# Overlapping the end of an FFN with the next block: per-sequence sum and LayerNorm inside the last attention slots, front of a state-space block beside the last MLP

## The chip, the cores and the metric

The kernel runs on one core of one Trainium2 chip. Its engines are TensorE (PE), VectorE (DVE), ScalarE (ACT), GpSimd (POOL) and SyncE (SP), which only issues DMAs here. They run their own instruction queues and meet at semaphores. The metric is the device time of one execution in microseconds; less is better.

## What is computed

Input x is 4 sequences of 512 tokens with 128 channels, all in f32. Four blocks follow one another, each with its own LayerNorm (without weights) and residual sum:

```python
x = x + gla(layernorm(x))       # gated linear attention
x = x + ffn(layernorm(x))       # the first FFN: 6 layers
x = x + mamba(layernorm(x))     # the state-space block
x = x + ffn(layernorm(x))       # the second FFN, same weights
```

A layer of the FFN, on its own stream x, is

```python
x = local_attention(shift_tokens(x)) @ Wo + x
xn = layernorm(shift_tokens(x)) * g + b
a, gate = split(xn @ W1 + b1)
x = (a * gelu(gate)) @ W2 + b2 + x
```

The state-space block, on the normed x, is

```python
x, z = split(x @ in_proj); x = silu(causal_conv4(x) + conv_b)
dt, B, C = split(x @ x_proj); delta = softplus(dt @ dt_proj + 2 * dt_b)
for each of 16 states n:  h = h * exp(delta * A[n]) + delta * x * B[n];  y += h * C[n]
out = ((y + x * D) * silu(z)) @ out_proj
```

## The kernel before

All activations lie transposed, channels on partitions and the tokens of a sequence along the row: `xm` (x_main) is the residual stream, `xf` (x_ffn) the stream of the running block, `[128, 4, 512]` each. The order of each engine's queue is written by hand; nothing is reordered.

**PSUM** has 8 banks of 512 f32: `proj_ps` (0, 1), `tr_ps` (2, 3), `s_ps` (4, 5), `o_ps` (6, 7). In the state-space block banks 6 and 7 are `front`, 0 and 1 hold the spread b, 3 the spread c, 2 and 0 or 1 the inputs, 4 and 5 the sums y.

**An FFN** is 24 iterations `it = 4 * layer + j` of a body over sequence j, and a body is four slots u = 0 to 3 of 128 tokens. The work is staggered: in slot u the q, k, v projections are those of slot u + 2 or u + 3, transposes and scores of slot u + 1, probs times values of slot u (`pe_pv`, L328), and the output projection of slot u - 1 (`pe_wo`, L363; `dve_wo` adds it to the stream). The MLP of the sequence before rides along: centering, variance and `act_rstd` in slot 0, the up projections (`pe_up`, L385 and L386) with gelu and `dve_hidden` in slots 1 and 2, the down projection (`pe_down`, L394, and `dve_down`) in slot 3. All of these use banks 6 and 7. The last body has no next slots to project, and after it come, by themselves, the last output projection and the whole MLP of sequence 3.

**The hand-over.** Then `dve_add(1)` adds `xf` to `xm` for four sequences (L1049), and `pe_ln`, `act_ln`, `dve_ln` with stage 2 normalize all four: centering (L987), square, one-column matmuls with the mean (L991), a square root on ACT (L1015), a reciprocal and a diagonal matrix on DVE (L1033, L1037), a matmul that spreads it (L997), the scale on DVE (L1028). SP fetches the state-space weights when the sums are done (L1189, L1191; 8 DMAs, `mamba_in` waits for them). POOL multiplies taps and input weights (L1491) and makes the skip diagonals (L1495).

**The state-space block** has a front for each sequence b: 8 convolution matmuls (L1209), silu into `mb_u` (L1317), two gate matmuls (L1216) and their silu (L1321), x_proj (L1223), the split of its result in three bf16 parts (`first_part`, `rest_part`, `middle_part`, `last_part`), dt_proj (L1232), and softplus by four rounds of a square on ACT (L1346) and a product on DVE (L1422). Then 16 steps n: PE spreads b and c (L1241, L1244), ACT makes the decay (L1360) and copies c (L1364), DVE makes the inputs (L1440) and scans (L1447), POOL multiplies by c (L1512), and PE sums (L1255). Step s = 16 b + n. The front of sequence b + 1 is worked off inside the steps of b: convolutions at n = 0, 2, 3, 4, gates at 5, silu on ACT after the decay and c of step 6 (the "silu visit"), x_proj at 6, dt_proj at 7.

In SBUF the FFN's and the state-space block's buffers share one region, one after the other.

## Time and profile before

| | |
|---|---|
| three runs | 3748.36, 3751.72, 3775.46 us |
| median | 3751.72 us |
| profiled execution | 3771.7 us, its span 3769.9 us |
| mean granted clock of TensorE | 0.967 |
| PE, DVE, ACT, POOL busy in the span | 92%, 78%, 72%, 72% |
| the stretch 1740 to 1764 us | DVE 5.26, ACT 5.54, POOL 0.00 us busy |

All times on the profile's clock are microseconds from the span's start. Busy time of PE is modelled and includes waiting in its pipeline. In a timeline, a row is one or several equal instructions, and the brackets say how long the engine had been idle before it and what released it. On PE a f32 matmul leaves two records, so x16 are eight matmuls. PEclk is the share of full clock that TensorE was granted: 1.00 is 2.4 GHz, 0.50 is 1.2 GHz.

### The profile page before, as it was taken

How to read it: one execution, taken by the hardware profiler on the slowest of the kernel's cores; microseconds unless marked ns; L12 is line 12 of the kernel's file. 1: busy time of each engine (PE TensorE's matmuls, PEld its weight loads, DVE VectorE, ACT ScalarE, POOL GpSimd, SP SyncE). 2: the span in 40 equal slices, each digit the busy share in tenths (PEclk: the TensorE clock that was granted, in tenths of full speed). 3: DMA queues.
4: the chain of work that ended last, by engine and by line, in shares of the span. 5: the costliest groups of instructions: out<-in, count | busy, mean ns of one | idle time of the engine just before them, and what ended most of it. 6: DMA issues, size and time to landing. Idle time of an engine off the chain costs nothing. (4 is left out here: it accounts for less than half of the span.)

```text
span 3769.9 us, 152591 instructions
## 1 busy us (share of the span) xinstructions
PE 3478.4 (92%) x62652; PEld 2492.0 (66%) x62652; DVE 2942.3 (78%) x4681; ACT 2729.4 (72%) x7144; POOL 2732.0 (72%) x3102
## 2 busy tenths in 40 slices
PE   8799999999999999997787799999999999999997
PEld 3477777777777777774232477777777777777774
DVE  7678888878878788783799688878888887878783
ACT  2477878777887778773656477877777787877774
POOL 4588878777878778781466587878787787878772
PEclk9899999999999999997899899999999999999998
DMA  1222333332333323221000133323332332323321
GB/s 41 57 74 74 80 77 76 80 77 70 84 77 75 80 72 81 75 73 40 0 1 1 45 76 74 84 74 76 78 77 72 84 79 68 87 72 76 77 73 37
DMA packets 182983, 252.03 MB, mean 67 GB/s; under 512 B 53396, under 2 KB 74520, under 8 KB 182168
## 3 DMA queue, kind: packets, MB, share of 16 engines
q1 hardware_dynamic: 182296, 242.31, 25.4%
q8 instruction: 500, 8.19, 1.0%
q14 instruction: 187, 1.53, 0.1%
HBM read 39.73 MB, written 1.05 MB: 11 GB/s over the span
## 5 line engine op out<-in xcount | busy, mean ns | idle before, releaser
L860 POOL TENSOR_TENSOR qk_rows<-rot_products 128x512 f32<-128x512 f32 x768 | 982.7, 1281 | 237.1 <-DVE rot_products L659 233.9
L659 DVE TENSOR_TENSOR rot_products<-psum,rot_scaled 128x1024 f32<-128x1024 f32 x768 | 936.7, 1220 | 156.8 <-ACT squares L470 132.9
L870 POOL TENSOR_TENSOR qk_rows<-qk_rows,rnorm 128x512 f32<-128x512 f32 x768 | 802.6, 1076 | 15.0
L266 PE MATMUL psum<-wqkv_hi,xs_hi 128*128 128x512 f32 x1152 | 561.0, 487 | 89.3 <-DVE rot_products L659 37.9
L470 ACT ACTIVATE squares<-psum 128x512 f32<-128x512 f32 x768 | 488.7, 637 | 46.1 <-PE psum L268 40.2
L661 DVE TENSOR_REDUCE sumsq<-squares 128x8 f32<-128x512 f32 x768 | 518.7, 675 | 0.0
L478 ACT ACTIVATE v_rows<-psum 128x512 f32<-128x512 f32 x384 | 228.2, 596 | 377.5 <-DMA v_pairs<-v_rows 203.2
L835 POOL TENSOR_TENSOR probs<-probs,rden 128x512 f32<-128x512 f32 x384 | 392.5, 1043 | 111.1 <-DVE rden L709 109.9
L328 PEld LDWEIGHTS psum<-probs_t,v_pairs 64*64 64x64 f32 x24576 | 394.0, 137 | 106.0 <-issue 105.5
L514 ACT ACTIVATE probs<-psum,minus_row_max 128x64 f32<-128x64 f32 x1536 | 458.7, 337 | 5.7 <-DVE minus_row_max L693 5.5
L268 PE MATMUL psum<-wqkv_hi,xs_lo 128*128 128x512 f32 x1152 | 461.4, 401 | 0.3 <-issue 0.3
L267 PE MATMUL psum<-wqkv_lo,xs_hi 128*128 128x512 f32 x1152 | 460.5, 400 | 0.0
L328 PE MATMUL psum<-probs_t,v_pairs 64*64 64x32 f32 x24576 | 421.4, 222 | 30.9 <-issue 27.2
L363 PEld LDWEIGHTS psum<-o_t,wo 128*128 128x128 f32 x3072 | 366.5, 194 | 87.6 <-ACT o_t L486 67.2
L363 PE MATMUL psum<-o_t,wo 128*128 128x128 f32 x3072 | 391.4, 281 | 28.5 <-ACT o_t L486 20.6
L279 PE MATMUL psum<-ident,qk_rows 128*128 128x128 f32 x3072 | 407.1, 276 | 0.7 <-ACT q_t L497 0.7
L279 PEld LDWEIGHTS psum<-ident,qk_rows 128*128 128x128 f32 x3072 | 362.1, 143 | 29.3 <-issue 3.4
L313 PEld LDWEIGHTS psum<-k_t,q_t 64*32 64x32 f32 x24576 | 268.5, 105 | 152.8 <-issue 152.7
L514 ACT ACTIVATION_READ_ACCUMULATOR probs<-psum,minus_row_max 128x1 f32 x1536 | 355.6, 231 | 0.0
L266 PEld LDWEIGHTS psum<-wqkv_hi,xs_hi 128*128 128x128 f32 x1152 | 219.3, 190 | 191.8 <-issue 115.3
L313 PE MATMUL psum<-k_t,q_t 64*32 64x64 f32 x24576 | 330.9, 224 | 1.6 <-issue 1.6
L693 DVE TENSOR_REDUCE minus_row_max<-psum 128x16 f32<-128x1024 f32 x192 | 234.3, 1221 | 113.3 <-PE psum L313 113.1
(163 smaller groups left out, 6020.9 us busy)
## 6 DMA issues: line engine op xcount, KB each, us to landing
v_pairs<-v_rows SPq DMA_DIRECT2D x3072, 64.0 KB, 2.0
wqkv_staged<-in_Wqkv SPq DMA_DIRECT2D x52, 384.0 KB, 3.8
wo<-in_Wo SPq DMA_DIRECT2D x12, 512.0 KB, 4.5
w<-in_W SPq DMA_DIRECT2D x12, 341.0 KB, 3.7
qk_scale<-in_qk_scale SPq DMA_DIRECT2D x12, 128.0 KB, 3.6
w<-in_W SPq DMA_DIRECT2D x12, 128.0 KB
rot_base<-in_rot SPq DMA_DIRECT2D x2, 512.0 KB, 3.7
mb_bc_pick<-in_mb_bc_pick SPq DMA_DIRECT2D x1, 1024.0 KB
```

The source lines that it names most:

```text
L266: nc.tensor.matmul(proj_ps[c % 2], xh, wh, start=True, stop=False)
L268: nc.tensor.matmul(proj_ps[c % 2], xl, wh, start=False, stop=True).then_inc(S["qkv_mm"], 1)
L279: last = nc.tensor.transpose(tr_ps[g % 2][:, i * P:(i + 1) * P], m["qk"][:, u % 2, (4 * g + i) * P:(4 * g + i + 1) * P], ident[:, :])
L313: last = nc.tensor.matmul(s_ps[par][WIN * w:WIN * w + WIN, 64 * hp:64 * hp + 64], m["qt"][rows, hp, WIN * w:WIN * w + WIN], m["kt"][rows, ...
L328: last = nc.tensor.matmul(o_ps[par][64 * j:64 * j + 64, P * (hp // 2) + WIN * w:P * (hp // 2) + WIN * w + WIN], m["vp"][rows, u % TILES, w ...
L363: last = nc.tensor.matmul(o_ps[0][:, 0:P], m["wo"][:, hp, :], m["ot"][:, hp, :], start=(hp == 0), stop=(hp == HP - 1))
L470: nc.scalar.activation(m["sq"][:, c % 2, :], proj_ps[c % 2], ACT.Square).then_inc(S["sq_done"], 1)
L514: last = nc.scalar.activation(m["p"][:, hp, 1, :], s_ps[1][:, 2 * WIN * hp:2 * WIN * (hp + 1)], ACT.Exp, bias=m["mx"][:, 1, hp:hp + 1], ac ...
L659: V.tensor_tensor(m["mm"][:, c % 2, :, :].rearrange("p a (h e) -> p a h e", e=DH), ps, cos_sin, ALU.mult)\
L661: V.tensor_reduce(m["ss"][:, HC * c:HC * c + HC], m["sq"][:, c % 2, :].rearrange("p (h e) -> p h e", e=DH), AX.X, ALU.add)\
L860: G.tensor_tensor(qk[:, c * CH:(c + 1) * CH].rearrange(half, a=2, e=DH // 2), cos, sin[:, :, ::-1, :], ALU.add)\
L870: G.tensor_tensor(part, part, m["rn"][:, u % 2, HC * c:HC * c + HC].unsqueeze(2) .to_broadcast([P, HC, DH]), ALU.mult).then_inc(S["rot_don ...
```

## The change

Sum and LayerNorm between the first FFN and the state-space block are done sequence by sequence, with new functions (`pe_norm_center`, `pe_norm_var`, `pe_norm_spread`, `act_norm_square`, `act_norm_seed`, `pool_norm`, `dve_sum`, `dve_norm_scale`). Those of sequence 0 stand in slots 2 and 3 of the last body, those of 1 and 2 among the tail of the FFN and the front of the state-space block, that of 3 in the first steps. The inverse square root is an Ln and an Exp of the four columns on ACT, one Newton step and the diagonal on POOL, in place of a square root on ACT and a reciprocal and a diagonal on DVE.

The output projection and MLP of the last sequence are interleaved with the front of sequence 0 of the state-space block, on banks 2 to 5, and the down and output projections in the last slot go to banks 5 and 4 behind the exponentials. The weights of the state-space block are fetched after the last k is transposed. In the block, silu stands in the middle of step 7 on ACT (in the decay, ahead of the copy of c), the gates with x_proj at step 6 on PE, `rest_part` and `last_part` one step later on DVE; for b = 0 the convolutions stand at steps 2 to 5. The weights, vectors, rotary tables, `o_t` and `xn_mlp` of the FFN keep their place for the whole kernel, the rotary base is loaded once, and `mb_tap_w` and `mb_dt_low` lie in other tiles. The functions of the block are renamed with `mb_`.

```diff
+            mb["wt"] = mb["taps"]
...
+            mb["xdt"] = mb["rest"][0:RANK, :]
...
+        tail_ps = ((s_ps[0], s_ps[1]), (tr_ps[0], tr_ps[1]), (s_ps[0], s_ps[1]))
...
+        def pe_norm_center(b, out):
+            nc.tensor.wait_ge(x_ready, 2 * B + b + 1)
+            wait(nc.tensor, ln_done[2], b)
+            nc.tensor.matmul(out, center[:, :], xm[:, b, :], start=True, stop=True).then_inc(N["center_mm"], 1)
+
+        def pe_norm_var(b, out):
+            nc.tensor.wait_ge(N["sq"], b + 1)
+            for t in range(TILES):
+                last = nc.tensor.matmul(out[:, t:t + 1], norm_sq[:, t * P:(t + 1) * P], mean[:, 0:1], start=True, stop=True)
+            last.then_inc(N["var_mm"], 1)
+
+        def pe_norm_spread(b, out):
+            nc.tensor.wait_ge(N["diag"], b + 1)
+            nc.tensor.matmul(out, mean[:, :], norm_sq[:, :], start=True, stop=True).then_inc(N["spread_mm"], 1)
+
...
+                if norm and u == 3:
+                    nc.tensor.wait_ge(S["exp1_done"], cnt(it, 1, u, 1))
+                    pe_down(it - 1, added_ - 1, s_ps[1])
+                    nc.tensor.wait_ge(S["sub_done"], cnt(it, 1, u, 1))
+                    pe_wo(it, u - 1, s_ps[0])
+                elif prev:
                     pe_wo(it, u - 1)
...
+                if norm and u == 3:
+                    pe_norm_spread(0, proj_ps[1])
                 if nxt:
                     pe_scores(it, u + 1, 0)
+                if norm and u == 2:
+                    pe_norm_center(0, proj_ps[0])
                 if proj:
                     pe_proj(it, u + 2, 4, two)
                 if mlp and u == 0:
...
+                if norm and u == 2:
+                    pe_norm_var(0, proj_ps[1])
...
+        def act_norm_square(b, src):
+            nc.scalar.wait_ge(N["center_mm"], b + 1)
+            wait(nc.scalar, N["spread_mm"], b)
+            nc.scalar.activation(norm_sq[:, :], src, ACT.Square).then_inc(N["sq"], 1)
+            nc.scalar.activation(xf[:, b, 1:1 + T], src, ACT.Copy).then_inc(N["centered"], 1)
+
+        def act_norm_seed(b, src):
+            nc.scalar.wait_ge(N["var_mm"], b + 1)
+            wait(nc.scalar, N["diag"], b)
+            nc.scalar.activation(norm_cols[:, 0, :], src[:, 0:TILES], ACT.Identity, bias=eps_t[:, :]).then_inc(N["var"], 1)
+            nc.scalar.activation(norm_cols[:, 1, :], src[:, 0:TILES], ACT.Ln, bias=eps_t[:, :]).then_inc(N["log"], 1)
+            nc.scalar.wait_ge(N["log"], b + 1)
+            nc.scalar.activation(norm_cols[:, 1, :], norm_cols[:, 1, :], ACT.Exp, scale=-0.5).then_inc(N["seed"], 1)
...
+        def dve_sum(b):
+            V.wait_ge(S["stream"], PHASE + b + 1)
+            for rows, x in stream(b):
+                last = V.tensor_tensor(xm[rows, b, :], xm[rows, b, :], x, ALU.add)
+            last.then_inc(x_ready, 1)
+
+        def dve_norm_scale(b, rs):
+            V.wait_ge(N["spread_mm"], b + 1)
+            V.wait_ge(N["centered"], b + 1)
+            V.memset(xpad[0:64, b, SHIFT - 1:SHIFT], 0.0).then_inc(ms["zero"], 1)
+            V.tensor_tensor(xf[:, b, 1:1 + T], xf[:, b, 1:1 + T], rs, ALU.mult).then_inc(ln_done[2], 1)
+
...
+                if norm and u == 2:
+                    dve_sum(0)
...
+                if norm and u == 3:
+                    dve_down(it - 1, s_ps[1])
+                    dve_wo(it, u - 1, s_ps[0])
+                    dve_norm_scale(0, proj_ps[1])
+                elif prev:
...
+                if norm and u >= 2:
+                    dve_sum(u - 1)
...
+        def pool_norm(b):
+            var, y, t_ = norm_cols[:, 0, :], norm_cols[:, 1, :], norm_cols[:, 2, :]
+            G.wait_ge(N["var"], b + 1)
+            G.wait_ge(N["seed"], b + 1)
+            G.tensor_tensor(t_, y, y, ALU.mult).then_inc(N["newton"], 1)
+            G.wait_ge(N["newton"], 4 * b + 1)
+            G.tensor_tensor(t_, t_, var, ALU.mult).then_inc(N["newton"], 1)
+            G.wait_ge(N["newton"], 4 * b + 2)
+            G.tensor_scalar(t_, t_, -0.5 * P, 1.5 * P, ALU.mult, ALU.add).then_inc(N["newton"], 1)
+            G.wait_ge(N["newton"], 4 * b + 3)
+            G.tensor_tensor(y, y, t_, ALU.mult).then_inc(N["newton"], 1)
+            G.wait_ge(N["newton"], 4 * b + 4)
+            G.tensor_tensor(norm_sq[:, :].rearrange("p (t q) -> p t q", t=TILES),
+                            ident[:, :].unsqueeze(1).to_broadcast([P, TILES, P]),
+                            y.unsqueeze(2).to_broadcast([P, TILES, P]), ALU.mult).then_inc(N["diag"], 1)
...
+                if norm and u == 2:
+                    pool_mamba_weights()
+                if norm and u == 3:
+                    pool_norm(0)
...
         def sp_mamba(sp):
-            sp.wait_ge(x_ready, 3 * B)
+            sp.wait_ge(S["qkT_mm"], cnt(PHASE, 4, 0))
+            sp.wait_ge(S["rot_done"], cnt(PHASE, QKC, 0))
...
+        def mb_conv(b, j, taps):
+            if 0 in taps:
+                T_.wait_ge(ms["zero"], b + 1)
+                T_.wait_ge(ln_done[2], b + 1)
...
         def pe_mamba():
...
+            e = PHASE - 1
+            pe_norm_center(1, proj_ps[0])
             mamba_in(T_)
-            T_.wait_ge(ln_done[2], B)
-            T_.wait_ge(ms["zero"], 1)
+            T_.wait_ge(S["oT_ev"], cnt(PHASE, 2, 0) - 1)
+            mb_conv(0, 0, (0, 1))
...
+            pe_wo(e, 3, s_ps[0])
+            mb_conv(0, 0, (2, 3))
+            pe_center(e, s_ps[0])
+            pe_norm_var(1, proj_ps[1])
+            mb_conv(0, 1, (0, 1))
...
+            pe_var(e, s_ps[1])
+            mb_conv(0, 1, (2, 3))
+            pe_norm_spread(1, proj_ps[1])
+            pe_tail_up(e, 0)
+            mb_gate(0, 0)
+            mb_gate(0, 1)
+            pe_tail_up(e, 1)
+            mb_x_proj(0)
+            pe_tail_up(e, 2)
+            pe_norm_center(2, proj_ps[0])
+            mb_dt_proj(0, 0)
+            mb_dt_proj(0, 1)
+            pe_tail_down(e)
+            pe_norm_var(2, proj_ps[1])
+            pe_norm_spread(2, proj_ps[1])
+            T_.wait_ge(N["centered"], 3)
+            mb_spread(0)
...
+                    if n == 0 and b == 0:
+                        T_.wait_ge(ms["delta"], 2)
+                        pe_norm_center(3, front[0])
+                    if n == 1 and b == 0:
+                        pe_norm_var(3, front[1])
+                    if n == 2 and b == 0:
+                        pe_norm_spread(3, front[1])
+                    if n == (2 if b == 0 else 0):
+                        if b == 0:
+                            T_.wait_ge(N["centered"], B)
+                        mb_conv(b + 1, 0, (0, 1))
+                    if n == (3 if b == 0 else 2):
+                        mb_conv(b + 1, 0, (2, 3))
+                    if n == (4 if b == 0 else 3):
+                        if b == 0:
+                            T_.wait_ge(ln_done[2], B)
+                        mb_conv(b + 1, 1, (0, 1))
+                    if n == (5 if b == 0 else 4):
+                        mb_conv(b + 1, 1, (2, 3))
                     if n == 6:
-                        x_proj(b + 1)
+                        mb_gate(b + 1, 0)
+                        mb_gate(b + 1, 1)
+                        mb_x_proj(b + 1)
                     if n == 7:
...
+                        mb_dt_proj(b + 1, 0)
+                        mb_dt_proj(b + 1, 1)
...
+            if n == 7 and b + 1 < B:
+                mb_silu(b + 1)
+                A_.preload_act_table_set("natural_log_exp_and_others")
...
         def act_mamba():
+            e = PHASE - 1
+            act_norm_square(1, proj_ps[0])
+            act_center(e, s_ps[0])
+            act_norm_seed(1, proj_ps[1])
+            act_rstd(e, s_ps[1])
             mamba_in(A_)
             A_.activation(mb["a"][:, :, :], mb["alog"][:, :, :], ACT.Exp).then_inc(ms["a1"], 1)
+            mb_silu(0)
+            act_gelu(e, 0, tail_ps[0][1])
+            act_gelu(e, 1, tail_ps[1][1])
+            mb_first_part(0)
+            act_gelu(e, 2, tail_ps[2][1])
             A_.wait_ge(ms["cols"], 2 + QUADS)
+            mb_middle_part(0)
             for j in range(2):
+                mb_dt_exp(0, j)
             for i in range(QUADS):
                 for j in range(2):
+                    mb_quad(0, i, j)
+                if i == 0:
+                    act_norm_square(2, proj_ps[0])
+                if i == 1:
+                    act_norm_seed(2, proj_ps[1])
             for j in range(2):
+                mb_relu_back(0, j)
...
+                if s == 1:
+                    act_norm_square(3, front[0])
+                if s == 2:
+                    act_norm_seed(3, front[1])
...
-                    if n == 6:
-                        silu(b + 1)
...
+            dve_wo(e, 3, s_ps[0])
+            dve_norm(e)
+            dve_norm_scale(1, proj_ps[1])
...
+            dve_hidden(e, 0, tail_ps[0][0])
+            dve_hidden(e, 1, tail_ps[1][0])
             rest_part(0)
+            dve_hidden(e, 2, tail_ps[2][0])
             last_part(0)
+            dve_down(e, tail_ps[1][0])
+            dve_sum(3)
             for i in range(QUADS):
...
+            dve_norm_scale(2, proj_ps[1])
...
-                if b + 1 < B and n == 7:
+                if b + 1 < B and n == 8:
                     rest_part(b + 1)
-                if b + 1 < B and n == 8:
+                if b + 1 < B and n == 9:
                     last_part(b + 1)
                 scan(s)
+                if s == 2:
+                    dve_norm_scale(3, front[1])
                 if b > 0 and n == 0:
                     gated(b - 1)
...
+            pool_norm(1)
+            pool_norm(2)
...
+                if s == 1:
+                    pool_norm(3)
...
-            sp.wait_ge(x_ready, 4 * B)
-            sp.dma_start(m["rot"][:], a["rot"]).then_inc(rot_in, 16)
```

Names in the rows below: `o_t` is the attention output, `probs_t` the transposed probs, `v_pairs` the values, `mb_taps` the convolution weights, `mb_in_w` the gate weights.

PE from the last slot's probs times values on, before:

```order
L328 MATMUL psum<-probs_t,v_pairs 64x32 [waits d1_ev,stream,pT_ev,vp3]
L328 MATMUL psum<-probs_t,v_pairs 64x32 x63
L363 MATMUL psum<-o_t,wo 128x128 [waits oT_ev]
L363 MATMUL psum<-o_t,wo 128x128 x7
L369 MATMUL psum<-x_ffn,center 128x512 [waits d1_ev]
L373 MATMUL psum<-hidden,mean 128x512 [waits xc_ev]
L385 MATMUL psum<-xn_mlp,w 128x512 [waits xn2,d1_ev,w1_in,logv_done]
L386 MATMUL psum<-xn_mlp,w 128x512
L385 MATMUL psum<-xn_mlp,w 128x512 [waits d1_ev,gelu_done,h_done]
L386 MATMUL psum<-xn_mlp,w 128x512
L385 MATMUL psum<-xn_mlp,w 85x512 [waits gelu_done,h_done]
```

and in the change:

```order
L429 MATMUL psum<-x_main,center 128x512 [waits ln2_done,x_ready]
L1329 MATMUL psum<-x_ffn,mb_taps 128x512 [waits m_zero,oT_ev,ln2_done,m_weights,m_in]
L1329 MATMUL psum<-x_ffn,mb_taps 128x512
L372 MATMUL psum<-o_t,wo 128x128 [waits oT_ev,d1_ev]
L372 MATMUL psum<-o_t,wo 128x128 x7
L1329 MATMUL psum<-x_ffn,mb_taps 128x512 x2
L378 MATMUL psum<-x_ffn,center 128x512 [waits d1_ev]
L434 MATMUL psum<-mean,norm_sq 128x1 [waits norm_sq]
L434 MATMUL psum<-mean,norm_sq 128x1 x3
L1329 MATMUL psum<-x_ffn,mb_taps 128x512 [waits ln2_done,m_zero]
L1329 MATMUL psum<-x_ffn,mb_taps 128x512
L382 MATMUL psum<-hidden,mean 128x512 [waits xc_ev,stream]
```

Between probs times values and the up projections stand now the centering of sequence 1 and the convolutions of the state-space block, with the tail's output projection, centering and variance among them.

POOL from the last two products of probs on, before:

```order
L835 TENSOR_TENSOR probs<-probs,rden 128x8x64 [waits den_done]
L835 TENSOR_TENSOR probs<-probs,rden 128x8x64
L835 TENSOR_TENSOR probs<-probs,rden 128x8x64 [waits den_done]
L835 TENSOR_TENSOR probs<-probs,rden 128x8x64
L1491 TENSOR_TENSOR mb_tap_w<-mb_taps,mb_in_w 128x1024 [waits m_in]
L1495 TENSOR_TENSOR mb_skip_diag<-ident,mb_cols 128x128 x2
L1501 TENSOR_TENSOR mb_du<-mb_delta,mb_u 128x512 [waits m_delta] x2
```

and in the change:

```order
L934 TENSOR_TENSOR probs<-probs,rden 128x8x64 [waits den_done]
L934 TENSOR_TENSOR probs<-probs,rden 128x8x64
L1674 TENSOR_TENSOR mb_taps<-mb_taps,mb_in_w 128x1024 [waits m_in]
L1678 TENSOR_TENSOR mb_skip_diag<-ident,mb_cols 128x128 x2
L934 TENSOR_TENSOR probs<-probs,rden 128x8x64 [waits den_done]
L934 TENSOR_TENSOR probs<-probs,rden 128x8x64
L976 TENSOR_TENSOR norm_cols<-norm_cols 128x4 [waits norm_seed,norm_var]
L978 TENSOR_TENSOR norm_cols<-norm_cols 128x4 [waits norm_newton]
L980 ISA
L980 TENSOR_SCALAR norm_cols<-norm_cols 128x4 [waits norm_newton]
L982 TENSOR_TENSOR norm_cols<-norm_cols 128x4 [waits norm_newton]
L984 TENSOR_TENSOR norm_sq<-ident,norm_cols 128x512 [waits norm_newton]
```

The weights moved ahead of the last product of probs, and the new LayerNorm operations follow, with an ISA row ahead of the first TENSOR_SCALAR.

ACT around the silu visit of sequence 1, before:

```order
L1360 ACTIVATE mb_decay<-mb_delta,mb_a 128x512 [waits m_h] x2
L1364 ACTIVATE mb_c<-psum 128x512 [waits m_hc,m_c_mm]
L1317 ACT_TABLE_LOAD [waits m_du,m_skip_mm]
L1317 ACTIVATE mb_u<-psum,mb_cols 128x512 [waits m_conv_mm]
L1317 ACTIVATE mb_u<-psum,mb_cols 128x512
L1321 ACTIVATE mb_z<-psum 128x512 [waits m_z_mm] x2
L1360 ACT_TABLE_LOAD
L1360 ACTIVATE mb_decay<-mb_delta,mb_a 128x512 [waits m_h] x2
L1364 ACTIVATE mb_c<-psum 128x512 [waits m_hc,m_c_mm]
```

and in the change:

```order
L1511 ACTIVATE mb_decay<-mb_delta,mb_a 128x512 [waits m_h] x2
L1518 ACTIVATE mb_c<-psum 128x512 [waits m_hc,m_c_mm]
L1511 ACTIVATE mb_decay<-mb_delta,mb_a 128x512 [waits m_h] x2
L1468 ACT_TABLE_LOAD [waits m_du,m_skip_mm]
L1468 ACTIVATE mb_u<-psum,mb_cols 128x512 [waits m_conv_mm]
L1468 ACTIVATE mb_u<-psum,mb_cols 128x512
L1472 ACTIVATE mb_z<-psum 128x512 [waits m_z_mm] x2
L1515 ACT_TABLE_LOAD
L1518 ACTIVATE mb_c<-psum 128x512 [waits m_hc,m_c_mm]
```

The table load and the four silu operations moved behind one more pair of decays and ahead of its copy of c.

## Rows read from the trace of the kernel before

**Rows 1.** The page, engines' busy time
```profile
PE 3478.4 (92%) x62652; PEld 2492.0 (66%) x62652; DVE 2942.3 (78%) x4681; ACT 2729.4 (72%) x7144; POOL 2732.0 (72%) x3102
```

**Rows 2.** Busy time of each engine, two stretches
```profile
1740.00:1764.00 24.00, 13.42 (x20) 4.24 (x20) 5.26 (x8) 5.54 (x8) 0.00 (x0) 0.79 0.00 0
1764.00:1822.00 58.00, 33.61 (x82) 15.45 (x83) 22.77 (x42) 28.19 (x46) 6.46 (x5) 0.71 0.12 37
```

**Rows 3.** Timeline of DVE (start, duration, what, idle time before)
```profile
1763.72 5.63 DVE L1049 TENSOR_TENSOR x_main<-x_main,x_ffn 64x512 f32<-64x512 f32 x8
1779.01 2.71 DVE L1037 SCALAR_TENSOR_TENSOR gelu<-ident,ln_cols 128x512 f32<-128x512 f32 x1
1821.59 2.32 DVE L1447 TENSOR_TENSOR_SCAN mb_h<-mb_decay,psum 128x512 f32<-128x512 f32 x2
```

**Rows 4.** Timeline of PE in the last two slots
```profile
1716.27 1.71 PE L328 MATMUL psum<-probs_t,v_pairs 64*64 64x32 f32 x103 [0.86 <-DVE hidden L735]
...
1721.32 3.78 PE L363 MATMUL psum<-o_t,wo 128*128 128x128 f32 x16 [2.52 <-ACT o_t L486]
1725.79 5.13 PE L394 MATMUL psum<-hidden,w 128*128 128x512 f32 x6 [0.68 <-DVE x_ffn L720]
```

**Rows 5.** Timeline of PE, matmul prices at 2.4 GHz
```profile
1735.91 2.05 PE L363 MATMUL psum<-o_t,wo 128*128 128x128 f32 x16 [1.22 <-ACT o_t L486]
...
1788.97 7.11 PE L1209 MATMUL psum<-x_ffn,mb_tap_w 128*128 128x512 f32 x16 [1.01 <-DVE x_ffn L1400]
...
2100.07 0.95 PE L991 MATMUL psum<-mean,hidden 128*128 128x1 f32 x8
```

**Rows 6.** Granted clock in two stretches (PE busy, PEclk, DMA)
```profile
1720.00:1724.00 4.00, 2.68 (x12) 0.52 0.00 0
1732.00:1736.00 4.00, 2.16 (x129) 1.00 0.01 4
```

**Rows 7.** Timeline of ACT, prices of its pieces
```profile
1772.02 0.59 ACT L1012 ACTIVATE hidden<-psum 128x512 f32<-128x512 f32 x1
...
1777.21 1.28 ACT L1015 ACT_TABLE_LOAD   x1
1778.50 0.57 ACT L1015 ACTIVATE ln_cols<-psum,eps_t 128x4 f32<-128x4 f32 x3
...
1806.11 0.69 ACT L1336 ACTIVATE mb_dt_relu<-psum,mb_dt_bias 128x512 f32<-128x512 f32 x1
...
1811.04 1.28 ACT L1346 ACTIVATE psum<-mb_dt_exp,mb_quad 128x512 f32<-128x512 f32 x2
```

**Rows 8.** Timeline of POOL, a small operation and the weights
```profile
1699.22 0.25 POOL L827 TENSOR_TENSOR newton_t<-newton_t,minus_sumsq 128x32 f32<-128x32 f32 x1
...
1778.83 2.35 POOL L1491 TENSOR_TENSOR mb_tap_w<-mb_taps,mb_in_w 128x1024 f32<-128x1024 f32 x1 [55.41 <-DMA mb_bc_pick<-in_mb_bc_pick]
```

**Rows 9.** Timeline of SP, DMA issues
```profile
1701.01 11.91 SPq L916 DMA_DIRECT2D v_pairs<-v_rows  x16
1769.39 0.33 SPq L1189 DMA_DIRECT2D mb_taps<-in_mb_taps  x1
```

**Rows 10.** Timeline of POOL, then its line L1166
```profile
39.78 1.26 POOL L1166 TENSOR_TENSOR gla_state_q<-gla_state,gla_q 128x512 f32<-128x512 f32 x1 [39.34 <-DVE gla_state L1146]
L1166 POOLq MODIFY_POOL_CONFIG  x2: 11/11/11, 0.7 to 0.8; - x2
```

**Rows 11.** Timeline of DVE around the first silu visit
```profile
1828.04 1.30 DVE L1440 TENSOR_TENSOR psum<-psum,mb_du 128x512 f32<-128x512 f32 x2 [0.71 <-PE psum L1241]
...
1842.99 2.32 DVE L1447 TENSOR_TENSOR_SCAN mb_h<-mb_decay,psum 128x512 f32<-128x512 f32 x2
1847.74 1.30 DVE L1440 TENSOR_TENSOR psum<-psum,mb_du 128x512 f32<-128x512 f32 x2 [2.43 <-PE psum L1241]
1851.63 0.69 DVE L1410 TENSOR_TENSOR mb_rest<-psum,mb_parts 64x512 f32<-64x512 f32 x1 [2.59 <-ACT mb_parts L1328]
...
1860.20 2.32 DVE L1447 TENSOR_TENSOR_SCAN mb_h<-mb_decay,psum 128x512 f32<-128x512 f32 x2
```

418 lines of the change are left out of this document (211 added, 207 removed).

## Prediction

> **What bounds the kernel now.** I read the page first [rows 1], then busy time by stretches, then the timelines of the stretch where the first FFN ends. Over the span every engine has 72% or more of busy time, so an average shows no bound. The hand-over from the first FFN to the state-space block is different: from 1740 to 1764 POOL does nothing and DVE and ACT are busy a fifth of the time; from 1764 to 1822 no engine reaches 60% [rows 2]. The reader is to see one step after another there: the sums of all four sequences start at 1763.72, and the first scan at 1821.59 [rows 3]. Each step's latency counts, and the engines take turns. The change interleaves this chain with itself, so its price is read from the latencies of one path, and not from busy time. Inside the state-space block DVE is the bound, except for two waits at each silu visit, of 2.43 and 2.59 us [rows 11].
>
> I follow the path of the changed program with durations of this trace, on its clock, and ask at which time its first scan starts; before it is 1821.59. Two records of PE are one f32 matmul; sixteen in 7.11 us are 0.89 us for one of 512 columns. An output projection is 2.05, the four one-column matmuls of a LayerNorm 0.95 [rows 5].
>
> **Third slot of the last sequence (u = 2).** The added centering of sequence 0 puts 0.9 us on PE ahead of the last up projection. On ACT the square and the copy (two of 0.59, overlapping to 1.1 [rows 7]) stand ahead of the exponentials. PE waits for the square before the one-column matmuls. Probs times values, which started at 1716.27 [rows 4], so starts near 1719.3 and ends at 1721.7. The three narrow operations of the seed (about 0.25 each [rows 7], no table load here) delay the eviction behind them to 1723.8. The sums on DVE fall into its idle time.
>
> **Fourth slot (u = 3).** PE goes on with the down projection and the output projection, which now have banks of their own and don't wait for DVE. Before, they ran at 1.2 GHz (clock 0.52 [rows 6]), took 5.13 and 3.78 us and had 2.52 us of idle time before them [rows 4]. PE still idles and does light one-column work near 1717 to 1719, so I keep the low prices: 1721.8 + 5.1 + 3.8 = 1730.7. The transposes of probs (1.0) and the spread of sequence 0 (0.9) follow, to 1732.7. POOL must be ready by 1731.7. Its new load of weights waits for eight DMAs, and SP can't issue these before its sixteen v_pairs issues end, at 1712.9 [rows 9]. Before, the time from the first issue (1769.39) to POOL's start on them (1778.83) was 9.4 us [rows 8, 9], so POOL starts at 1722.4. The weights take 4.0 in all, probs 2.0, four small operations 0.33 apart 1.3, the diagonal 1.2: 1731.0, so 0.7 us to spare. At 2.4 GHz PE would gain four microseconds and hand them to this wait, so the clock decides little here. Probs times values ends at 1734.8, as before. The third slot's delay is absorbed.
>
> **From 1734.8.** PE is continuous: four centerings, variances and spreads at 0.89 (3.6), eight convolution taps (7.1), an output projection (2.05) and one-column matmuls (0.95) give 13.7, to 1748.6 with the small gaps. ACT and POOL deliver the MLP's rstd and the second diagonal in this time (the seed ends near 1744.5, and 2.6 us on POOL later is 1747.1). Then come two up projections, two gates, x_proj and the third up projection (9 us), a centering, and the first dt matmul (1.8), to 1759.5. Silu, gelu and their two table loads on ACT run beside that. Before, ACT took 4.9 us from the first relu (1806.11) to the first square (1811.04) [rows 7], and 10.55 from there to the scan [rows 3]. Now square and copy of sequence 2 (1.1) and its seed stand among the squares. That seed has two table loads of 1.28 and three narrow operations: 3.5 [rows 7]. The waits that they fill give back 0.4. The sum is 1759.5 + 4.9 + 10.55 + 1.1 + 3.5 - 0.4 = 1779.2. The scaling of sequence 2 hides under POOL's mb_du. For DVE beside POOL I add 1.5 us: the diagonal that took 2.71 us began 0.2 us after a POOL operation [rows 3, 8], and its like take 0.69. **Front: the scan starts at 1780.7, a gain of 41 us.** The old separate LayerNorm, the wait for the DMAs and the tail are gone in that; what is late next is ACT's chain of squares.
>
> The Trainium skill has a rule that speaks against the four added loads: ScalarE: Activation LUTs, What ACT_TABLE_LOAD costs, gives each switch 1.28 us and about 1.38 more for a drain. The trace shows the first part, and an operation 0.01 us behind the load [rows 7]. By the page the four would cost 5.5 us more, and the forecast would be 3712; the row decides.
>
> **Inside the block.** Silu moves from behind step 6 to the middle of step 7 on ACT, the gates on PE from step 5 to 6, and the rest part on DVE from 7 to 8. Before, DVE needed 17.2 us from scan 6 (1842.99) to scan 9 (1860.20) [rows 11]. Now inputs and scan of step 7 are served before ACT leaves. DVE is free at 1848.7; the visit gives c and the next b at 1850.8 (table load, two u, gate, z, x_proj: the same pieces as before). That is one wait of 2.1 for two of 5.0 together: 14.2 us, **3.0 less**, in sequences 1 and 2. In sequence 0 the LayerNorm of sequence 3 is put in. Its seed (3.5 after about 6.8 from the scan's start), POOL's 2.6 and the spread of 1.0 let the scale on DVE end at 14.7, where scan 2 ended at 9.2. That is 5.5 for a wait of 0.71 before [rows 11]; the visit gives 2.8 back: **2.0 more**. Inside: 3.0 + 3.0 - 2.0 = 4 us gained.
>
> **Free edits.** Buffers that stay live, the single load of rot and the earlier loads of FFN weights save nothing: nothing at the start of the second FFN waited for them. The body of both FFNs is unchanged.
>
> **Sum.** 41 + 4 = 45 us. The profiled execution took 3771.7 us for a span of 3769.9, 20 over the median of 3751.72; the difference of 45 is taken from either, so 3726.7 for such an execution and **3707** for the median.
>
> **Rivals.** (a) *The clock.* The interleaved stretch from 1734.8 has 24 us of PE work at the high level. Near 1721 PE had idled 2.5 us and the clock was 0.52 [rows 4, 6]; a low level through this stretch costs 3.78 / 2.05 = 1.84 times, 20 us more, a gain of 25: 3727. For it speaks that half of the old hand-over ran low; against it, that the new order leaves no such gap.
> (b) *POOL's code.* The new order has an ISA row before the first TENSOR_SCALAR on POOL, as before the first arithmetic of the kernel. There, configuring took 11 ns, at 0.8 us, and the next operation came at 39.78 because DVE was awaited [rows 10]. So a load behind it costs between 0 and 39 us. It would hold pool_norm(0), the spread, and probs times values behind it on PE. All of it but the 0.7 to spare is lost: from 3707 to 3745. I take 0, as no row shows any. The Trainium skill has the rule (GPSIMD Engine Reference, Instruction dispatch): the first call into newly loaded code costs about 6 us. By it the time would be 3712, and no row here shows it.
> (c) *Slower.* The same mechanism ends on the other side if the load in the middle of the run takes more than 46 us, since all engines stand still: 3752 and up. The bound of 39 speaks against it.
> (d) *The block loses.* If each silu visit gains nothing (PE's gates now hold b of step 8, and ACT's copy of c is late) and LayerNorm 3 costs 8, the block loses 8 and the gain is 33: 3719.
>
> **Chances.** Forecast 0.67, (a) 0.12, (b) 0.07, (c) 0.02, (d) 0.09, others 0.03. One per cent is 37.5 us, about what a measurement of this kernel can tell from no change; its three runs lie 27 us apart. Faster by over 1%: the forecast and part of (b), less what misses the bound by some microseconds, 0.70. Within 1%: (a), (d) and the rest, 0.27. Slower: 0.03. Range: from 3695 (no contention, 4 us more in the block, and a median some microseconds low) to 3730, which takes in (a), (d) and (b) up to 23 us.
>
> **What the profile will show.** The first scan near 1781; PE busy without a gap over 1 us from 1735 to 1759; the DMA landed by 1722.5; probs times values of the last slot unmoved; two table loads between the squares; the old waits of 2.43 and 2.59 replaced by one near 2 us at step 8; a DVE wait near 5 us behind scan 2 of sequence 0. It is wrong if POOL stands before its TENSOR_SCALAR, if PEclk is 0.5 past 1735, or if the second FFN's length differs.

## The result, and the profile after

The changed kernel takes 3709.42 us, the median of 4 runs (3706.15 to 3711.19), against 3750.04 for the kernel before in the same session (3748.03 to 3775.46, 4 runs). The ratio is 0.9881, 95% interval 0.9855 to 0.9907: 40.6 us or 1.2% faster. The forecast was 3707 with a range of 3695 to 3730. The profiled execution took 3706.15 us with a span of 3704.4; that of before was a long one, 3771.7.

The page's busy line answers to [rows 1]: the same work, 31 us less of it on PE, whose records are longer where its clock is low.

```profile
PE 3447.7 (93%) x62652; PEld 2472.5 (67%) x62652; DVE 2934.0 (79%) x4676; ACT 2727.1 (74%) x7154; POOL 2739.4 (74%) x3122
```

To set the traces side by side I count from row maxima of the attention on DVE, 96 in each FFN. The stretch from the 94th to the 97th row maximum holds the end of the first FFN, the hand-over, the state-space block and the start of the second FFN. It took 464.5 us before and 414.5 after. From the 94th row maximum to the first scan it was 138.2 and 95.0, from the first scan to the last 266.4 and 260.6, and from there to the 97th row maximum 60.0 and 58.9. Times of after are 13 us earlier than those of before for the same work ahead of the change.

Busy time in stretches, columns as in [rows 2] (length, then PE, PEld, DVE, ACT, POOL, granted clock, DMA share, GB/s):

```profile
1721.00:1750.00 29.00, 28.16 (x100) 12.81 (x92) 7.23 (x19) 17.92 (x30) 1.83 (x5) 1.00 0.11 32
1750.00:1765.20 15.20, 6.20 (x17) 3.22 (x18) 10.69 (x18) 14.37 (x25) 4.34 (x7) 0.66 0.05 12
1704.00:1711.00 7.00, 6.42 (x138) 5.63 (x139) 3.44 (x6) 5.49 (x24) 0.08 (x1) 0.58 0.65 209
```

Where [rows 2] had two stretches, 82 us together, in which no engine reached 60%, there are now 29 us in which PE is busy 97% at a clock of 1.00, and 15 us in which ACT is busy 95%. So the bound passes from PE to ACT at 1750.

The last two slots, PE (start, duration, what, idle time before in brackets; answers to [rows 4]):

```profile
1705.89 3.64 PE L335 MATMUL psum<-probs_t,v_pairs 64*64 64x32 f32 x128
1709.46 4.07 PE L403 MATMUL psum<-hidden,w 128*128 128x512 f32 x6
1713.37 1.95 PE L372 MATMUL psum<-o_t,wo 128*128 128x128 f32 x16
1716.03 1.09 PE L301 MATMUL psum<-ident,probs 128*128 128x128 f32 x8 [0.71 <-POOL probs L934]
1718.15 1.12 PE L439 MATMUL psum<-norm_sq,mean 128*128 128x512 f32 x2 [1.03 <-POOL norm_sq L984]
1719.21 2.07 PE L335 MATMUL psum<-probs_t,v_pairs 64*64 64x32 f32 x128
```

And POOL beside it:

```profile
1710.92 2.34 POOL L1674 TENSOR_TENSOR mb_taps<-mb_taps,mb_in_w 128x1024 f32<-128x1024 f32 x1 [15.69 <-DMA mb_bc_pick<-in_mb_bc_pick]
1713.94 2.04 POOL L934 TENSOR_TENSOR probs<-probs,rden 128x512 f32<-128x512 f32 x2
...
1716.21 0.20 POOL L978 TENSOR_TENSOR norm_cols<-norm_cols 128x4 f32<-128x4 f32 x1
1716.50 0.19 POOL L980 TENSOR_SCALAR norm_cols<-norm_cols 128x4 f32<-128x4 f32 x1
1716.78 0.20 POOL L982 TENSOR_TENSOR norm_cols<-norm_cols 128x4 f32<-128x4 f32 x1
```

PE waits twice for POOL (in the third profile of this kernel once, 0.92 us), whose queue was held by the eight DMAs until 1710.92. The code of POOL was configured here, and no time was lost to it:

```profile
L980 POOLq MODIFY_POOL_CONFIG  x2: 11/11/11, 1716.4 to 1716.4; - x2
```

The TENSOR_SCALAR behind it began 0.29 us after the operation before, and the next one 0.28 us after that: whatever was loaded, no operation waited for it. After 1719.21 PE has no gap above 0.25 us until 1749.4.

Then ACT is the chain (timeline of ACT; answers to [rows 7]):

```profile
1750.76 1.28 ACT L1497 ACTIVATE psum<-mb_dt_exp,mb_quad 128x512 f32<-128x512 f32 x2
...
1754.72 1.28 ACT L598 ACT_TABLE_LOAD   x1
1756.01 0.26 ACT L598 ACTIVATE norm_cols<-psum,eps_t 128x4 f32<-128x4 f32 x1
1756.29 1.28 ACT L600 ACT_TABLE_LOAD   x1
```

And DVE ahead of the block and in it (answers to [rows 3, 11]):

```profile
1758.40 1.30 DVE L1597 SCALAR_TENSOR_TENSOR mb_poly<-psum,mb_poly 128x512 f32<-128x512 f32 x2 [3.17 <-ACT psum L1497]
...
1762.55 0.68 DVE L832 TENSOR_TENSOR x_ffn<-x_ffn,psum 128x512 f32<-128x512 f32 x1
...
1765.25 2.32 DVE L1622 TENSOR_TENSOR_SCAN mb_h<-mb_decay,psum 128x512 f32<-128x512 f32 x2
...
1772.08 2.32 DVE L1622 TENSOR_TENSOR_SCAN mb_h<-mb_decay,psum 128x512 f32<-128x512 f32 x2
1779.00 0.68 DVE L832 TENSOR_TENSOR x_ffn<-x_ffn,psum 128x512 f32<-128x512 f32 x1 [4.60 <-issue]
...
1799.82 1.30 DVE L1615 TENSOR_TENSOR psum<-psum,mb_du 128x512 f32<-128x512 f32 x2 [2.21 <-PE psum L1361]
```

The first scan starts at 1765.25. Behind scan 2 DVE waits 4.60 us for the matmul that spreads the scale of sequence 3, and at step 8 it waits 2.21 us for B, once, where it waited 2.43 and 2.59 at this visit before.

### The profile page after: what moved, and what is told of

Its sections match the earlier page's. It is cut to its first block and busy times, and to the rows that moved or that the text cites. A ratio compares the mean times of both kernels' runs of the same rounds, so it can differ in the third digit from the quotient of the medians.

```text
span 3704.4 us, 152641 instructions
## 1 busy us (share of the span) xinstructions
PE 3447.7 (93%) x62652; PEld 2472.5 (67%) x62652; DVE 2934.0 (79%) x4676; ACT 2727.1 (74%) x7154; POOL 2739.4 (74%) x3122
## 3 DMA queue, kind: packets, MB, share of 16 engines
q1 hardware_dynamic: 182152, 241.78, 26.2%
## 5 line engine op out<-in xcount | busy, mean ns | idle before, releaser
L934 POOL TENSOR_TENSOR probs<-probs,rden 128x512 f32<-128x512 f32 x384 | 393.3, 1045 | 92.4 <-DVE rden L786 91.5
```

## The experiments

All medians are given with that of the kernel before in the same session. "Front" is the 94th row maximum to the first scan, "scans" the first scan to the last, "stretch" the 94th to the 97th row maximum, all in us and from the one profiled execution of each.

| run | median (runs) | before (runs) | ratio (95%) | front | scans | stretch |
|---|---|---|---|---|---|---|
| first result | 3709.42 (4) | 3750.04 (4) | 0.9881 (0.9855-0.9907) | 95.0 | 260.6 | 414.5 |
| ctl_before | 3738.97 (12) | 3740.90 (23) | 0.9994 (0.9979-1.0009) | 135.3 | 266.4 | 460.8 |
| ctl_after | 3699.91 (6) | 3740.90 | 0.9893 (0.9875-0.9911) | 95.4 | 260.6 | 414.9 |
| silu_alone | 3737.43 (12) | 3740.90 | 0.9986 (0.9972-1.0001) | 134.9 | 257.5 | 450.7 |
| old_silu | 3710.54 (6) | 3740.90 | 0.9921 (0.9902-0.9939) | 99.3 | 270.8 | 429.7 |
| tail_first | 3716.41 (4) | 3749.84 (9) | 0.9920 (0.9898-0.9943) | 108.6 | 261.3 | 428.8 |
| one_set | 3702.28 (4) | 3749.84 | 0.9867 (0.9843-0.9890) | 92.8 | 258.0 | 410.6 |
| weights_late | 3701.79 (4) | 3749.84 | 0.9883 (0.9860-0.9907) | 92.3 | 263.2 | 415.2 |
| best1 | 3695.69 (5) | 3749.84 | 0.9862 (0.9842-0.9881) | 89.6 | 259.0 | 407.4 |
| best2b | 3683.10 (6) | 3733.72 (17) | 0.9868 (0.9845-0.9891) | 91.5 | 255.6 | 406.6 |
| silu_again2 | 3727.60 (12) | 3733.72 | 0.9980 (0.9967-0.9994) | 135.3 | 256.7 | 451.7 |
| after_again2 | 3686.57 (6) | 3733.72 | 0.9873 (0.9852-0.9893) | 93.7 | 262.0 | 414.5 |

tail_first, one_set, weights_late and best1 ran in a session in which the changed kernel did not. Their medians can be set against it only through the ratios to the kernel before; what else is said of them below comes from their profiles, one of each.

### The two kernels again: ctl_before, ctl_after, after_again2

No edit.

> The kernel before, unchanged. The profiled execution of before took 3771.7 us, 22 over its other runs, and the two profiles differ by 66 us where the medians differ by 40.6. From the 94th row maximum of the first FFN to the first of the second the profiles differ by 50.0 us (464.5 against 414.5). Theory: the slow execution was slow in the FFNs (its first FFN took 13.8 us more than in the profile of the change), and the hand-over and block take 464 us again, the median gain of 40.6 then being partly lost in the FFNs. Rival: the hand-over itself was slow in that execution, and takes 455 us here, so that the difference is the 41 of the medians.

> The change, unchanged, as the reference for the runs beside it on the same chip. Both theories expect 40 us under before (ratio 0.989) and 414 to 416 us from the 94th row maximum of the first FFN to the first of the second.

> The changed kernel once more, in the same session as the kernel of the three edits with the loosened SiLU visit, to be compared with it. Expected 40 us below the kernel before, within 5, and the stretch from the 94th to the 97th row maximum at 414 to 416 us; if TensorE's clock falls once more between the slots and the convolutions, as it did in the run with the old SiLU visit, the first scan comes 4 to 5 us later there.

The change is worth 41.0 and 47.2 us in the two later sessions, and it was 40.6 in the first; the last is 2 us outside what was expected of after_again2. The stretch of ctl_before, 460.8 us, lies between what the theory and the rival gave (464 and 455): some 4 of the 50 us between the first two profiles belonged to that one execution. The stretch of the changed kernel repeats within 0.4 us in three profiles. That of before does not quite (464.5 and 460.8), since its front does not: 138.2 in the first profile, and 135.3, 134.9 and 135.3 in three others with the same front. So the front's gain is 40 to 42 us rather than the 43 of the first pair. What varies more is the time outside. From the first to the 94th row maximum, where no kernel here changes the order of work, the profiles lie between 1511.0 and 1527.6 us, and from the 97th to the last between 1535.7 and 1563.1. Over the 59 executions of the second session, time and mean granted clock within a kernel go together: 2.4 us less for each 0.001 of clock, with a correlation of -0.68. A single time therefore tells nothing about a few microseconds; the stretch tells more.

One part of the time outside differs beyond its scatter. The first row maximum starts 154.4 to 155.8 us into the four profiles with the front and buffers of the kernel before, and 155.5 to 158.0 us into the nine with those of the change: 1.6 us later on average, 1.1 of it ahead of the first instruction of the linear attention. No run takes apart which of the changed buffers and loads costs that.

### The moved SiLU visit: silu_alone, silu_again2, old_silu

silu_alone is the kernel before with this part alone, and silu_again2 is the same kernel; old_silu is the changed kernel with it undone (the same edit backwards, with sequence 0's gates at step 6 and those of the others at step 5).

```
 PE    gates of the next sequence: step 5 -> 6, beside x_proj
 ACT   silu(b + 1) and the table preload: behind step 6 ->
       into step 7, between its decays and its copy of c
 DVE   rest_part: step 7 -> 8;  last_part: step 8 -> 9
```

> The kernel before with the silu visit alone moved: gates at step 6, silu in the middle of step 7, rest and last part one step later. Theory (the visit leaves DVE one wait where it had two): the block gets 3 x 2.7 to 3 x 4.2 = 8 to 13 us shorter, 3740 us. Rival (the visit pays only in the changed block, whose convolutions stand later, or the wait is only moved): within 2 us of before.

> The change with the silu visit undone: silu on ACT behind step 6, gates on PE at step 5 (at 6 for sequence 0, whose last convolution stands at 5), rest and last part at steps 7 and 8. Theory: 8 to 13 us over the change, the front's part of the gain stays at 43. Rival (the visit gives nothing): as the change.

> The kernel before with the SiLU visit moved and nothing else, a second time. The first time the traces put the stretch from the 94th to the 97th row maximum at 450.7 us against 460.8 of the kernel before, 10.1 us less, while the median time was 1.5 us less in 12 runs of each. Theory: the 10.1 us are real (8.0 to 8.9 of them are in the scans, 2.7 for each of three visits), and the median was off by the scatter of TensorE's clock in the two MLP stretches, whose lengths differ by up to 16 us between runs of one and the same code: then a new set of runs gives 4 to 10 us less than the kernel before. Rival: the time is given back outside the stretch: then it is within 3 us again.

DVE ahead of scan 8 in silu_alone, the place of the two waits of [rows 11]:

```profile
1845.73 1.30 DVE L1440 TENSOR_TENSOR psum<-psum,mb_du 128x512 f32<-128x512 f32 x2 [2.11 <-PE psum L1241]
...
1847.79 2.33 DVE L1447 TENSOR_TENSOR_SCAN mb_h<-mb_decay,psum 128x512 f32<-128x512 f32 x2
```

And in old_silu, where the convolutions of sequence 1 stand a step later:

```profile
1810.25 1.30 DVE L1615 TENSOR_TENSOR psum<-psum,mb_du 128x512 f32<-128x512 f32 x2 [0.34 <-PE psum L1361]
1817.75 0.69 DVE L1585 TENSOR_TENSOR mb_rest<-psum,mb_parts 64x512 f32<-64x512 f32 x1 [6.20 <-ACT mb_parts L1480]
```

One wait of 2.1 us takes the place of two that sum to 5.0. From scan 0 to scan 9 silu_alone needs 35.9 us against 38.6, 2.7 less, and the same in sequences 1 and 2: the three visits give 8.0 us at step 41, and the stretch is 9 to 10 us shorter. In the changed kernel undoing the part costs 10.2 us of scans: 3.7 in sequence 0, where the old visit beside LayerNorm 3 becomes one wait of 6.20 us, 2.7 in each of the next two, and 1.3 between scans 16 and 22, which is the clock (see below) and not the visit. Of the whole time silu_alone gave 3.5 us against the runs of before, less than its theory and more than its rival, and silu_again2 6.1 us, inside the 4 to 10 expected; the intervals reach from 0.01% slower to 0.33% faster. The stretch's 9 to 10 us stand just within both; whether some of it is given back in the FFNs is not settled by 24 runs. The median of old_silu is 10.6 us above that of ctl_after, as its theory has it; its stretch is 15 us longer, since its front lost some 4 us too.

old_silu also shows the clock rival at work in the front. PE's timeline there, and the clock in stretches of 4 us:

```profile
1716.98 2.75 PE L335 MATMUL psum<-probs_t,v_pairs 64*64 64x32 f32 x128
1719.66 4.10 PE L403 MATMUL psum<-hidden,w 128*128 128x512 f32 x6
...
1727.86 1.09 PE L301 MATMUL psum<-ident,probs 128*128 128x128 f32 x8 [2.31 <-POOL probs L934]
1729.99 2.08 PE L439 MATMUL psum<-norm_sq,mean 128*128 128x512 f32 x2 [1.03 <-POOL norm_sq L984]
1731.99 3.64 PE L335 MATMUL psum<-probs_t,v_pairs 64*64 64x32 f32 x128
```

```profile
1726.00:1730.00 4.00, 1.10 (x9) 0.87 (x9) 0.17 (x1) 1.08 (x2) 3.60 (x7) 0.88 0.00 0
1730.00:1734.00 4.00, 4.00 (x78) 2.50 (x82) 1.83 (x4) 0.00 (x0) 0.00 (x0) 0.50 0.02 4
1734.00:1738.00 4.00, 4.00 (x67) 2.67 (x61) 0.28 (x5) 1.41 (x3) 0.00 (x0) 0.50 0.00 0
```

The code up to here is that of the changed kernel. But PE was faster in the third slot (probabilities times values 2.75 us for 3.64; the down projection took 4.10 for 4.07) and done 1.2 us sooner, counted from the 96th row maximum, and POOL's weights started 0.4 us later. So PE waited 2.31 us for POOL instead of 0.71, and then the clock fell to 0.50, 1.2 GHz. The spread took 2.08 us for 1.12, probabilities times values 3.64 for 2.07, the centering 2.07 for 1.12 and the first two taps 2.81 for 1.95, 4.3 us more in these four rows. With POOL's 0.4 that is the delay of the first scan, 4.7 us from the 96th row maximum (66.6 against 61.9). In the changed kernel the clock was low ahead of the wait, 0.58 from 1704 to 1711, where slowness only shortens the wait. In these two executions the speed of PE ahead of the wait was worth nothing, and behind it all of it counted. one_set below shows the same once more: a wait of 3.11 us, then a clock of 0.50 from 1720 to 1724. In the other seven profiles of kernels with the change PE waited 1.04 us or less at a time here, and probabilities times values took 2.07 us.

### The interleaving: tail_first

The changed kernel with the last MLP run to its end before the front of sequence 0; sums and LayerNorms in the slots stay.

```
 PE   - conv(0,0) wo center conv(0,0) conv(0,1) var conv(0,1) ...
      - up(0) gates up(1) x_proj up(2) ... dt down
      + wo center var ... up(0) up(1) up(2) down
      + conv(0,0) conv(0,1) gates x_proj ... dt
 ACT, DVE: silu(0), first/rest/last part behind the three gelus
```

> The changed kernel with one part undone: on TensorE, ScalarE and VectorE the last MLP runs to its end before the first convolution, SiLU and projections of sequence 0; the sum and LayerNorm of sequences 0 and 1 and the moved SiLU visit stay. It measures what the interleaving alone brings. Theory: the front's own chain takes 17.1 us from its first convolution to the first Relu (1788.97 to 1806.11 in the kernel before) and the last MLP's 27.5 us from the end of probabilities times values (1734.6 to 1762.1 there); one after the other from 1721.2 they give the first Relu 44.6 us later, at 1765.8 on the changed kernel's clock, where it stands at 1745.8. So from the 94th row maximum to the first scan 95 becomes 112 to 115 us, and the run is 17 to 20 us slower than the changed kernel's control. Rival: the first scan waits mostly for the slots, the sum and ScalarE's table loads, which stay as they are; then 0 to 8 us slower.

The front is 13.3 us longer than the changed kernel's 95.0 to 95.4, between the two expectations and nearer to the theory. By the ratios (0.9920 against 0.9873 to 0.9893) the run is 10 to 18 us slower, which no more than bears this out. It took both in series, as the theory has it, but each was shorter than in the kernel before:

```profile
1740.81 2.84 PE L423 MATMUL psum<-hidden,w 128*128 128x512 f32 x6 [1.56 <-DVE hidden L812]
1746.68 7.14 PE L1329 MATMUL psum<-x_ffn,mb_taps 128*128 128x512 f32 x16 [3.03 <-DVE x_main L825]
1754.60 1.98 PE L1336 MATMUL psum<-x_ffn,mb_in_w 128*128 128x512 f32 x4 [0.78 <-ACT mb_u L1469]
```

From the end of probabilities times values (1721.6) to that of the down projection (1743.6) it is 22 us for 27.5, and from the first convolution to the first Relu (1761.03) 14.4 for 17.1: the table load for SiLU stands ahead of the convolutions (1739.99), where it stood behind them before (1796.16), and the up projections follow each other without waits. A wait of 3.03 us for the last residual of the MLP is between. So of the front's 40 to 42 us, 13 to 15 come from the interleaving (108.6 against 93.7 to 95.4), and the other 27 (135.3 against 108.6) from the sum and LayerNorms in the slots and all that came with them, the earlier DMAs and separate banks among it. No run takes these 27 apart.

### Table loads: one_set

```
             mb_middle_part(0)
+            A_.preload_act_table_set("natural_log_exp_and_others")
             for j in range(2):
                 mb_dt_exp(0, j)
```

> The changed kernel with one instruction more: before the Exp of delta of sequence 0, ScalarE is asked for the table set that holds Exp, Ln and Square, so that the LayerNorm seeds of sequences 2 and 3 (lines 598 and 600 there) need no loads of their own. Theory: the four loads of 1.28 us that stand there go. Two of them are in ScalarE's chain to the first scan: 2.56 us earlier, 95.0 to 92.5 us from the 94th row maximum. The other two are inside VectorE's wait of 4.60 us behind scan 2, which falls to about 2.0. Together 5.1 us faster than the changed kernel's control. By the Trainium skill, ScalarE: Activation LUTs, Table sets, one set serves these functions, which speaks for it. Rival: other waits take over in both places (the polynomial's partners on VectorE, the sequence's other squares), and it is within 1 us.

The loads go (ACT, from the first Exp's preparation on):

```profile
1751.17 1.28 ACT L1535 ACT_TABLE_LOAD   x1
...
1760.50 0.25 ACT L598 ACTIVATE norm_cols<-psum,eps_t 128x4 f32<-128x4 f32 x1
1760.78 0.20 ACT L600 ACTIVATE norm_cols<-norm_cols 128x4 f32<-128x4 f32 x1
```

From the middle part on ACT to the first scan it is 17.9 us (1750.52 to 1768.44) against 20.6 (1744.63 to 1765.25), 2.7 less. The wait behind scan 2 is 1.46 us instead of 4.60:

```profile
1779.05 0.68 DVE L832 TENSOR_TENSOR x_ffn<-x_ffn,psum 128x512 f32<-128x512 f32 x1 [1.46 <-issue]
```

The stretch is 3.9 to 4.3 us shorter; the theory's 5.1 lacks about 1 us, which PE lost ahead of it: it waited 3.11 us for POOL in this execution and probabilities times values took 2.87. The Trainium skill (ScalarE: Activation LUTs, Table sets: the hidden batching unit) says that this set has both exp and ln, one load instead of two. The trace agrees: Ln and Exp, and Square and Relu with them, run here behind one load, where the compiler's own choice had cost two loads in each seed of sequences 2 and 3. By the ratios (0.9867 against 0.9873 to 0.9893) the run isn't separated from the changed kernel.

### GpSimd's order: weights_late

```
-                if norm and u == 2:
-                    pool_mamba_weights()
                 if norm and u == 3:
                     pool_norm(0)
+                    pool_mamba_weights()
```

> The changed kernel with GpSimd's products of the convolution's weights (2.35 us and 0.75 us) behind the last probabilities and the LayerNorm of sequence 0 instead of ahead of them. Theory: the last probabilities start at the weights' place, TensorE's waits of 0.71 us for the probabilities and 1.03 us for the LayerNorm's diagonal go, and the weights are still ready before the first convolution: 1.7 us faster, the first scan 93.3 us after the 94th row maximum. With the waits gone TensorE's granted clock stays at 1.00 from probabilities times values on, whereas the run with the old SiLU visit had 0.50 there for about 8 us. Rival: the waits for the denominators or for the weights at the first convolution take their place, and it is within 0.5 us; or the clock falls there again, and the first scan comes 3 to 5 us later.

POOL no longer stands at the DMA with the last probabilities behind it. They start 5.7 us after the 96th row maximum (1701.24), not 10.6:

```profile
1706.91 2.04 POOL L934 TENSOR_TENSOR probs<-probs,rden 128x512 f32<-128x512 f32 x2 [13.75 <-DVE rden L786]
...
1711.03 2.35 POOL L1673 TENSOR_TENSOR mb_taps<-mb_taps,mb_in_w 128x1024 f32<-128x1024 f32 x1
```

PE's two waits are gone, the clock is 1.00 behind them, and the first scan comes 59.9 us after the 96th row maximum for 61.9 (60.9 in the third profile of the same kernel). But the scans take 2.6 us more and the stretch is no shorter. The first convolution of sequence 1 met the low clock, 3.62 us where the changed kernel shows 2.63 and 2.67 in two profiles (3.24 in the third):

```profile
1774.61 3.62 PE L1328 MATMUL psum<-x_ffn,mb_taps 128*128 128x512 f32 x4
...
1780.47 1.88 PE L1328 MATMUL psum<-x_ffn,mb_taps 128*128 128x512 f32 x4
```

and PE did not catch up. A step with a convolution is 3.87 us of work on PE at the high clock (from one convolution to the next, 1780.47 to 1784.34) while DVE needs 3.42, so a delay of PE stays until the visit. after_again2 shows the same with the changed kernel's own code: it lost 1.5 us between scans 16 and 22, where the convolutions of sequence 2 stand. Its clock there (after_again2, then ctl_after, the stretch around scan 16 and the one behind it):

```profile
1836.00:1840.00 4.00, 2.13 (x4) 0.72 (x5) 4.00 (x6) 1.45 (x2) 3.37 (x4) 0.77 0.00 0
1840.00:1844.00 4.00, 4.00 (x10) 1.88 (x9) 3.21 (x6) 1.81 (x3) 2.17 (x2) 0.80 0.00 0
```

```profile
1837.00:1841.00 4.00, 3.75 (x6) 1.25 (x6) 4.00 (x6) 2.49 (x4) 4.00 (x5) 0.59 0.00 0
1841.00:1845.00 4.00, 3.19 (x9) 1.39 (x9) 4.00 (x6) 2.12 (x5) 3.38 (x3) 0.99 0.00 0
```

Scan 16 is at 1838.33 and at 1842.61. PE is the lightly loaded engine in the last steps of a sequence, and a stretch of low clock follows. In ctl_after it came ahead of scan 16 and the clock was back at 0.99 when the convolutions began; in after_again2 it came with them, and DVE waited for PE. All thirteen profiles sort by this. Where the clock was 1.00 in the 4 us from scan 16 or 32 on, the six steps took 23.3 us, and where it was 0.57 to 0.69, 24.6 to 24.9. Three of these rows, from scan 16 of the kernel before, scan 16 of silu_again2 and scan 32 of old_silu:

```profile
1890.10:1894.10 4.00, 4.00 (x8) 1.82 (x7) 3.84 (x6) 1.82 (x3) 3.22 (x3) 0.59 0.00 0
1870.00:1874.00 4.00, 4.00 (x8) 1.58 (x7) 3.21 (x5) 1.81 (x3) 3.22 (x3) 0.57 0.00 0
1927.98:1931.98 4.00, 4.00 (x11) 1.61 (x10) 4.00 (x6) 1.93 (x3) 3.23 (x3) 1.00 0.00 0
```

The six steps took 24.9, 24.9 and 23.3 us, and DVE (the third figure behind the length) is busy throughout only in the last. The first and the last kernel have the gates at step 5, the second at step 6, so the place of the gates doesn't decide it. weights_late lost in both places, 1.2 us by scan 8 and 1.5 more by scan 22, 2.6 in all at the end. So the gain is there at its place and lost at the next.

### Together, and the visit loosened: best1, best2b

best1 is one_set and weights_late, and on DVE one number more:

```
-                if s == 2:
+                if s == 3:
                     dve_norm_scale(3, front[1])
```

> The changed kernel with three edits at once: the table set asked for ahead, the convolution's weights behind the LayerNorm of sequence 0 on GpSimd, and VectorE's product with the LayerNorm's scale of sequence 3 behind scan 3 instead of behind scan 2. Theory: 2.6 and 1.7 us ahead of the first scan, and VectorE's wait of 4.60 us in the first visits gone altogether: 8 to 9 us faster than the changed kernel's control. Rival: the edits share their gain, since TensorE's convolutions of sequence 1 then start a step later and the wait shows at the next step; then 5 to 6 us.

The stretch is 407.4 us, 7.1 to 7.5 less than the changed kernel's, between what theory and rival gave. The front gives its part (57.0 us from the 96th row maximum for 61.9 or 60.9), and the wait behind scan 2 is gone. The rival's mechanism shows beside it: steps 3 to 6 take 4.4, 3.9, 3.9 and 3.9 us, since PE is the bound there, so scan 7 comes at 26.2 us after scan 0 for 30.1 in ctl_after, and from scan 0 to scan 63 only 1.6 us are left of it. The other 2.3 went to the same low clock: scans 16 to 22 took 24.9 us for 23.3, and scans 32 to 38 took 24.8 for 23.3, 3.1 us too long, of which 0.8 came back behind.

best2b adds to best1:

```
 ACT  step 7: decays, silu u, copy c, silu z, preload (c was last)
      first_part behind the decays of step 8; middle_part at step 9
 PE   step 6: gates, B and C of step 8, x_proj; dt_proj step 7 -> 8
 DVE  rest_part and last_part behind scans 8 and 9 (were ahead)
```

> The kernel of the three edits with the SiLU visit loosened: ScalarE copies C of step 7 between the SiLUs of u and of z instead of behind the table load, and the projection's copies go behind the decay of step 8; TensorE broadcasts B and C of step 8 between the gates and the projection, and the projection of dt goes a step later; VectorE takes the remainders behind the scans of steps 8 and 9. Theory: what is left of a visit, 6.6 us from scan 7 to scan 8 against 3.42 us elsewhere, is VectorE waiting 2.21 us for B of step 8 behind the gates and the projection, and then a remainder of 0.69 us in the way. B of step 8 then lands at the end of scan 6, so the step is 4.1 to 4.4 us long: 2.4 us less in each of three visits, 7 us less from the first scan to the last than with the three edits alone (259.0 us), and 3 to 7 us less in all. Rival: ScalarE's own chain of two table loads, four SiLUs and two decays sets the visit, and what TensorE gives back is lost to it: within 1 us.

```profile
1788.63 1.27 DVE L1620 TENSOR_TENSOR psum<-psum,mb_du 128x512 f32<-128x512 f32 x2
1790.69 2.33 DVE L1627 TENSOR_TENSOR_SCAN mb_h<-mb_decay,psum 128x512 f32<-128x512 f32 x2 [0.79 <-DVE psum L1620]
```

The wait of 2.2 us is gone and step 7 to 8 takes 4.3 us, as forecast. But the remainders now cost their time a step later, 4.5 us from scan 9 to scan 10, so a visit gives 1.4 us rather than 2.4, and the scans 3.4 rather than 7. Its median is 3.5 us below that of the changed kernel in the same session, and its ratio, 0.9868 against 0.9873, does not separate them; nor does best1's. What speaks for both is the stretch, 7 to 8 us shorter in the one profile of each than in the three of the changed kernel.

## Why the prediction was right

**Third and fourth slot.** Right, and for the reason given, with two errors that cancel. On before's clock (12.7 us later) the weights start at 1723.7 (1722.4 said), since from the first DMA issue (1700.08 in the trace of after) to POOL's start it was 10.8 us and not 9.4; but they took 3.0 us and not 4.0, so the diagonal is ready at 1730.8 (1731.0 said). Probabilities times values starts at 1731.9 (1732.7 said). The down projection and the output projection took 4.07 and 1.95 us, not 5.1 and 3.8, and the time went to POOL, as the prediction said that it would. That POOL sets this slot is shown by weights_late, where both waits vanish; how much time it sets varies, 2.0 us against two profiles of the changed kernel and 1.0 against the third.

**PE's continuous stretch.** Right: no gap above 0.25 us from 1719.2 to 1749.4, and clock 1.00. The clock rival fell for the changed kernel in three profiles, but that is a matter of where PE's clock is low and not of the order alone: with the same code up to there, old_silu paid 4.3 us for it, a fifth of the 20 that the rival named, since the clock came back after some 8 us.

**ACT's chain.** Right: squares at 1763.5 on that clock (1764.4 said), 14.5 us to the scan (14.75 said). The row's 1.28 per load held: the next operation begins 0.01 us behind a load, and one_set gained 2.7 us for two loads. So the drain of 1.38 us that the Trainium skill gives (ScalarE: Activation LUTs, What ACT_TABLE_LOAD costs), which would have made it 5.3, is not there.

**The front as a whole** was forecast at 41 and measured 40 to 43. In the first pair its scan came at 1778.0 on before's clock, 2.7 us ahead of the 1780.7 said. Of these, 0.9 were won by the squares and 0.3 behind them, and 1.5 are the term for DVE beside POOL. That term isn't there: with POOL busy beside them, the products at 1758.40 took 1.30 us for two, as in the kernel before, and the scaling at 1762.55 took 0.68. Why the one diagonal took 2.71 us in the kernel before stays open.

**POOL's code.** Rivals (b) and (c) fell with the rows at 1716.4 and 1716.50. The Trainium skill (GPSIMD Engine Reference, Instruction dispatch) gives about 6 us for the first call into newly loaded code. The trace doesn't agree for this operation: the TENSOR_SCALAR starts 0.1 us behind the second MODIFY_POOL_CONFIG.

**Inside the block.** The direction of both terms was right. Sequence 0 cost 2.7 us more (2.0 said; its wait of 4.60 is the 5 forecast). Sequences 1 and 2 gained 4.2 each where 3.0 was said, but only 2.7 of it is the visit. The other 1.5 lie in the first six steps of each sequence, 24.9 us in both sequences of both profiles of the kernel before and 23.3 in five of six cases of the changed one, and there they follow the clock and not the order, as the rows above show. So the visits and LayerNorm 3 together gave 2.7 us, less than the 4 said, and the clock brought the sum to 5.8 (4.4 in the third profile). That the block came out above the forecast is luck; whether the changed order makes the good case likelier can't be told from so few.

**The sum.** 45 us forecast; the stretch gave 46 to 50, the medians 40.6, 41.0 and 47.2. By the profiles the front gives 40 to 42, the block 2.7 and up to 3.1 more by the clock, and the start of the kernel takes 1.6 back: 41 to 46. The prediction put the edits to buffers and loads at nothing. At the start of the second FFN that held (58.8 to 58.9 us from the last scan in three profiles, for 59.1 and 60.0 before); at the start of the kernel it did not. What is left between the profiles and the medians is within the FFNs' own scatter, 17 us in the first and 27 in the second; that a few microseconds are given back there was neither shown nor excluded.

## What to carry to other kernels

When a serial hand-over is folded into the work before it, follow one path with durations of the old trace and ask of each engine's queue what stands behind a DMA wait: here the whole slot hung on POOL holding still for weights that were ready almost 9 us before their first convolution. Undo it in a run of its own, as weights_late does. Then look for the engine with the least slack in the next stage, since in these runs a gain upstream was kept only where PE didn't meet its low clock there. Before a few microseconds are put down to an edit, look at the granted clock of the same steps in every profile: here 1.5 us per sequence came and went with it in kernels of either order. Read small effects from a marked stretch of the trace, and large ones from medians.

## What was not expected of the hardware

- Two profiles with the same code up to there differ in where PE's clock is low (0.58 ahead of the wait in the changed kernel, 0.50 behind it in old_silu), and the cost goes from nothing to 4.3 us by that alone.
- PE's low clock around the end of a sequence costs nothing or 1.3 to 1.6 us in the next one, by whether it is back (1.00) or not (0.57 to 0.69) in the 4 us from its first scan; weights_late lost 1.5 us there and 1.2 in sequence 0, more than the 2 it had gained.
- MODIFY_POOL_CONFIG in the middle of the kernel (two records of 11 ns at 1716.4) held nothing up: the TENSOR_SCALAR behind it started at 1716.50 and took 0.19 us.
- Left to itself the compiler put two loads of 1.28 us into each of the LayerNorm seeds of sequences 2 and 3 although one set serves all of it; one line took out these four.
- The same FFN code took 1511.0 to 1527.6 us in one stretch and 1535.7 to 1563.1 in the other, over the profiles of this case.
